# A fused Perceiver block: the scan stage's accumulation, gates and the next group's preparation moved to other rounds

## The reference

```
# 1 cross attention, 16 heads of 16, 256 keys of ctx per sequence, with a key mask, then x @ Wproj + bproj
# 2 Mamba block on the result
xn = layernorm(x);  xz = xn @ in_proj_w.T;  xi, z = xz[..., :512], xz[..., 512:]
xc = silu(causal depthwise conv of 4 taps(xi) + conv_b)
xp = xc @ x_proj_w.T                       # 1 dt column, 16 of B, 16 of C
delta = softplus(xp[..., :1] * dt_w + dt_b)
h_t = exp(delta_t * A) * h_{t-1} + delta_t * B_t * xc_t      # 512 channels x 16 states, 64 steps
y   = sum over states of h_t * C_t, + xc * D_skip
x   = x + (y * silu(z)) @ out_proj_w.T
# 3 feed-forward, 1024 inside, weights in {-1, 0, 1} times a scale, activations rounded to 8-bit steps per row
```

## Time and profile before

| | |
|---|---|
| Median of 3 runs | 426.24 us (425.74, 426.24 and 870.03) |
| Profiled execution | 425.23 us, of which the span of instructions is 423.4 us |
| Scan stage (first scan to last) | 191.7 to 371.4 us of the span |
| TensorE busy / ScalarE / VectorE / GpSimd | 364.6 / 276.4 / 350.2 / 280.5 us |
| Chain that ended last | PE 34%, DVE 28%, issue 15%, ACT 11%, POOL 10% |
| TensorE's granted clock, mean | 0.976 of full |

### The profile page before, as it was taken

The page is one execution under the profiler, slowest core; times in us unless marked ns, Lnnn a source line. Parts: engine busy times, 40 slices in busy tenths (PEclk is TensorE's granted clock), DMA queues, the critical chain, the costliest instruction groups (busy, mean ns, idle before and its releaser), DMA issues.

```text
span 423.4 us, 8649 instructions
## 1 busy us (share of the span) xinstructions
PE 364.6 (86%) x2868; PEld 246.3 (58%) x2868; DVE 350.2 (83%) x727; ACT 276.4 (65%) x592; POOL 280.5 (66%) x329
## 2 busy tenths in 40 slices
PE   3899999979998999887779889799889788789784
PEld 1556767666666764453446556464667566647443
DVE  1559889777898878859998999787899999988795
ACT  1267599659966982698765496838764665166564
POOL 0055566555748471449986779988799799986830
PEclk9999999999999999998998899989899999999989
DMA  6971011010100000049100000464000000000001
GB/s 200 395 303 52 2 50 52 2 50 2 52 2 0 3 2 0 2 115 267 21 2 0 2 2 28 133 151 116 0 2 2 0 2 0 2 0 2 12 26 63
DMA packets 22623, 22.41 MB, mean 53 GB/s; under 512 B 1042, under 2 KB 20242, under 8 KB 22068
## 3 DMA queue, kind: packets, MB, share of 16 engines
q1 hardware_dynamic: 22020, 21.39, 16.3%
q10 hardware_dynamic: 560, 0.48, 0.3%
HBM read 20.75 MB, written 1.12 MB: 52 GB/s over the span
## 4 chain that ended last, share of the span: by engine, by line
PE 34%; DVE 28%; issue 15%; ACT 11%; POOL 10%; DMA 1%; DVEq 1%; POOLq 0%; PEldq 0%; ACTq 0%
DVE both L1570 12%; PE ps L531 7%; POOL both L1865 6%; PE ps L745 4%; PE ps L500 3%; PE ps L735 3%; PE ps L483 3%; DVE xc L1536 2%; DVE both L1402 2%; PE ps L518 2%; PE ps L561 2%; ACT both L1000 2%; PE ps L548 2%; PE ps L704 2%; ACT both L1146 1%
## 5 line engine op out<-in xcount | busy, mean ns | idle before, releaser
L1865 POOL TENSOR_TENSOR both<-both 128x1024 f32<-128x1024 f32 x64 | 149.8, 2362 | 18.6 <-PE ps L745 12.5
L1570 DVE TENSOR_TENSOR_SCAN both<-both,ps 128x1024 f32<-128x1024 f32 x64 | 143.0, 2272 | 5.7 <-PE ps L735 5.7
L1811 POOL TENSOR_SCALAR both<-both,rden 128x256 f32<-128x256 f32 x128 | 61.7, 497 | 62.7 <-DVE rden L1409 62.6
L1160 ACT ACTIVATE both<-delta,a_neg 128x504 f32<-128x504 f32 x120 | 74.7, 704 | 10.9 <-DVE both L1570 10.9
L745 PE MATMUL ps<-con,both 128*128 128x128 f32 x512 | 74.5, 289 | 2.0 <-POOL both L1865 1.9
L1000 ACT ACTIVATE both<-both,negmax 128x256 f32<-128x256 f32 x128 | 63.3, 498 | 17.4 <-DVE negmax L1402 17.4
L745 PEld LDWEIGHTS ps<-con,both 128*128 128x128 f32 x512 | 58.1, 146 | 24.0 <-issue 19.2
L735 PE MATMUL ps<-both 32*128 32x256 f32 x512 | 47.2, 439 | 16.1 <-DVE both L1570 14.1
L1402 DVE CUSTOM_DVE_ANT_0 both<-ps,both 128x256 f32<-128x256 f32 x128 | 46.9, 418 | 6.7 <-PE ps L483 5.5
L735 PEld LDWEIGHTS ps<-both 32*128 32x128 f32 x512 | 20.6, 187 | 34.3 <-DVE both L1570 24.3
L531 PE MATMUL ps<-both 128*128 128x512 f32 x64 | 33.5, 648 | 8.0 <-DMA both<-in_ctx_t 6.6
(11 more groups left out here) (145 smaller groups left out, 603.4 us busy)
## 6 DMA issues: line engine op xcount, KB each, us to landing
both<-bounce SPq DMA_DIRECT2D x16, 512.0 KB, 5.5
both<-in_ctx_t SPq DMA_DIRECT2D x8, 512.0 KB, 3.4
both<-in_wg SPq DMA_DIRECT2D x1, 1024.0 KB, 8.5
both<-in_wu SPq DMA_DIRECT2D x1, 1024.0 KB, 10.9
both<-in_wd SPq DMA_DIRECT2D x1, 1024.0 KB, 12.9
win_sb<-in_win SPq DMA_DIRECT2D x1, 1024.0 KB, 14.8
resid<-in_x SPq DMA_DIRECT2D x1, 896.0 KB, 6.4
both<-in_wkv SPq DMA_DIRECT2D x1, 512.0 KB, 4.2
```

What stands on the lines that cost most here:

```text
L1160: act.activation(da[sl % 2].rearrange("p (a s n t) -> p a s n t", a=GT, n=HN, s=2)[:, :, :, n, 1:L], delta[:, idx % RING_D].rearrange("p ( ...
L1570: dve.tensor_tensor_scan(h_sb[:, hu % RING_H], da[e.slot % 2][:, e.tt * HU:(e.tt + 1) * HU], bank(inflow_bank(hu), 2), 0.0, ALU.mult, ALU. ...
L1811: pool.tensor_scalar(s, s, rden[:, u, q:q + 1], 1.0, ALU.mult, ALU.mult).then_inc(normed, 1)
L1865: pool.tensor_tensor(g_sb[:, hu % RING_G].rearrange("p (n s t) -> p s n t", n=HN, s=2), h_sb[:, hu % RING_H].rearrange("p (s n t) -> p s n ...
```

## The change

`LAG_ACC` goes from 5 to 4, and with it each accumulate stands one half earlier. In round k TensorE now has accumulate(2k - 4), in halves around phase 1 of the inflow, and accumulate(2k - 3) at the very end of the round, behind the projection; in a round with k % 4 == 1 (`block_ends`) the latter comes ahead of the projection. In a next_block round nothing stands between the two phases; `seed` and the whole accumulate(2k - 4) follow them. The gate goes behind scan 8i + 10 (hu % 8 == 2), where it was behind 8i + 11. VectorE's `u_of(3)` goes from behind scan 12 to behind scan 0, `convolve(1, 2)` and `(1, 3)` from behind 13 and 17 to 11 and 13, `copy_b` from 24 to 22, `u_of(4)` and `u_of(5)` from 26 and 34 to 28 and 35. TensorE's and ScalarE's work for group 1 moves with them. No computation is added or removed.

```diff
--- before.py
+++ after.py
@@ -57,7 +57,7 @@
 RING_H, RING_G, RING_X, RING_D = 4, 4, 6, 5
 INFLOW_BANKS = (2, 6, 0)
 Y_BANK, SPARE_BANK = 5, 4
-LAG_ACC = 5
+LAG_ACC = 4
 NT_ACT = 3
 
 
@@ -837,19 +837,23 @@
             project(t7)
             turn_u(0, 6, (z_sb, 1))
             for k in range(NB):
+                next_block, block_ends = k > 2 and k % 4 == 2, k % 4 == 1
                 inflow(k, 0)
                 if k == 1:
                     pe.wait_ge(z_late, count(1))
                     seed(0, (0, 1))
                 elif k == 2:
                     seed(0, (2, 3))
-                elif k > 2:
+                elif k > 2 and not next_block:
                     accumulate(2 * k - LAG_ACC, range(0, HN // 2))
                 inflow(k, 1)
-                next_block = k > 2 and k % 4 == 2
-                if k > 2:
+                if next_block:
+                    seed(k // 4, range(GT))
+                if next_block or k == 2:
+                    accumulate(2 * k - LAG_ACC)
+                elif k > 2:
                     accumulate(2 * k - LAG_ACC, range(HN // 2, HN))
-                if k >= 2 and not next_block:
+                if k > 2 and block_ends:
                     accumulate(2 * k - LAG_ACC + 1)
                 if k == 0:
                     turn_u(1, 1, (masked, NT * 16))
@@ -864,26 +868,26 @@
                     turn_u(2, SPARE_BANK, (conv_step, convolved(1, 0)))
                 if k == 4:
                     in_proj(1, 1, SPARE_BANK, (ut_act, 1))
+                if k == 5:
+                    in_proj(1, 2, SPARE_BANK, (conv_step, convolved(1, 1)))
                 if k == 6:
-                    in_proj(1, 2, SPARE_BANK, (conv_step, convolved(1, 1)))
+                    in_proj(1, 3, SPARE_BANK, (conv_step, convolved(1, 2)))
                 if k == 7:
-                    turn_u(3, SPARE_BANK, (conv_step, convolved(1, 2)))
-                if k == 8:
-                    in_proj(1, 3, SPARE_BANK, (ut_act, 2))
-                if k in (10, 11):
-                    x_proj(1, 2 * (k - 10), SPARE_BANK, (conv_step, convolved(1, 3)))
-                    x_proj(1, 2 * (k - 10) + 1, SPARE_BANK, (conv_step, convolved(1, 3)))
+                    turn_u(3, SPARE_BANK, (conv_step, convolved(1, 3)))
+                if k in (8, 9):
+                    x_proj(1, 2 * (k - 8), SPARE_BANK, (ut_act, 2))
+                    x_proj(1, 2 * (k - 8) + 1, SPARE_BANK, (ut_act, 2))
+                if k == 11:
+                    turn_b(1, SPARE_BANK, (bsb_ready, 2))
                 if k == 12:
-                    turn_b(1, SPARE_BANK, (bsb_ready, 2))
+                    in_proj(1, 4, SPARE_BANK, (bt_sb, 2))
                 if k == 13:
-                    in_proj(1, 4, SPARE_BANK, (bt_sb, 2))
+                    in_proj(1, 5, SPARE_BANK, (z_sb, NC))
                 if k == 14:
-                    turn_u(4, SPARE_BANK, (z_sb, NC))
+                    turn_u(4, SPARE_BANK, (z_sb, NC + 1))
                 if k == 15:
-                    in_proj(1, 5, SPARE_BANK, (ut_act, 3))
+                    in_proj(1, 6, SPARE_BANK, (ut_act, 3))
                 if k == 16:
-                    in_proj(1, 6, SPARE_BANK, (z_sb, NC + 1))
-                if k == 17:
                     in_proj(1, 7, SPARE_BANK, (z_sb, NC + 2))
                 if k == 18:
                     turn_u(5, SPARE_BANK, (z_sb, 2 * NC - 1))
@@ -913,10 +917,8 @@
                     turn_input(0, SPARE_BANK)
                 if k == 31:
                     turn_input(1, SPARE_BANK)
-                if next_block:
-                    seed(k // 4, range(GT))
+                if k >= 2 and not block_ends:
                     accumulate(2 * k - LAG_ACC + 1)
-            accumulate(NHU - 5)
             accumulate(NHU - 4)
             gates(0)
             up(0)
@@ -1224,29 +1226,30 @@
             silu_gates(0, slice(2, GT))
             tap_first(1)
             slot(3)
+            tap_first(2)
             half_slot(4, 0)
-            tap_first(2)
+            tap_first(3)
             half_slot(4, 1)
             copy_ut(3, SPARE_BANK)
-            half_slot(5, 0)
-            tap_first(3)
-            half_slot(5, 1)
             for c in range(NC):
                 silu_xc(1, c)
+            slot(5)
+            copy_pr(1, SPARE_BANK)
             slot(6)
-            copy_pr(1, SPARE_BANK)
-            slot(7)
             softplus(1, range(NC), dtb[:], (dt_loaded, 16))
+            half_slot(7, 0)
             copy_gates(1, 0, SPARE_BANK)
-            stage_xc(4, (z_sb, NC + 1 - 1))
+            half_slot(7, 1)
+            copy_gates(1, 1, SPARE_BANK)
+            stage_xc(4, (z_sb, NC + 2 - 1))
             half_slot(8, 0)
             copy_ut(4, SPARE_BANK)
             half_slot(8, 1)
-            copy_gates(1, 1, SPARE_BANK)
             copy_gates(1, 2, SPARE_BANK)
-            slot(9)
+            half_slot(9, 0)
             copy_gates(1, 3, SPARE_BANK)
             stage_xc(5, (z_sb, 2 * NC - 1))
+            half_slot(9, 1)
             silu_gates(1)
             copy_ut(5, SPARE_BANK)
             slot(10)
@@ -1709,15 +1712,14 @@
                 scan(hu)
                 if hu == 0:
                     copy_late_gate()
-                if hu == 12:
                     u_of(3)
-                if hu in (5, 9, 13, 17):
-                    convolve(1, (5, 9, 13, 17).index(hu))
-                if hu in (26, 34, 41, 49):
-                    u_of(NC + (26, 34, 41, 49).index(hu))
-                if hu % (NH * GT) == 3 and hu > NH * GT:
+                if hu % (NH * GT) == 2 and hu > NH * GT:
                     gate(hu // (NH * GT) - 1)
-                if hu == 24:
+                if hu in (5, 9, 11, 13):
+                    convolve(1, (5, 9, 11, 13).index(hu))
+                if hu in (28, 35, 41, 49):
+                    u_of(NC + (28, 35, 41, 49).index(hu))
+                if hu == 22:
                     copy_b(1, SPARE_BANK)
                 if hu == 47:
                     add_scan(0, 0)
```

## The result

The changed kernel took 414.97 us, the median of 4 runs (414.41 to 417.95). The kernel before took 428.85 us beside it (425.74 to 870.03). The ratio is 0.9738, 95% interval [0.9701, 0.9774]: faster. It leaves out the single execution of 870.03 us, which lies far from all others; what lifts the median above the 426.24 us shown earlier is the fourth execution, of 431.46 us. The profiled execution took 414.41 us, its span 412.6 us, against 425.23 and 423.4.

The account below looks back on a forecast made before the run. The hand-written order was taken as the bound, VectorE's waits ahead of the first statistics as the gain: 16.0 - 5.6 - 0.6 = 9.8, less 0.9 for the clock, 8.9 off 425.23, plus 0.7 to the median: 417.0 us, range 412.5 to 424.

Parts of the forecast that it names:

- The waits removed: On VectorE, gate waits (2.3 us), first tap (0.8), u_of(4) (3.13) and u_of(5) (2.56) go; ceiling of gain 16.0 us.
- The waits put in: Ahead of VectorE's scans: waits of 5.0 us left, 5.6 with 0.1 for each of six.
- The walk: Rounds from scan 4 on, timed with measured start-to-start times; sum 16.0 - 5.6 - 0.6 = 9.8 us gained.
- Scan 4: Early scan stage: scan 4 keeps its place at 201.8; u_of(3) fills the 0.60 us ahead, leaving 0.2.
- TensorE's clock: Rounds 6, 7 and 14: new idle times may bring 1.2 GHz stretches, 0 to 4 us; 0.9 taken off.
- What a halved stretch costs: Behind idle times of rounds 6, 7 and 14: 1.0 to 1.5 us, of which round 14's would count whole.
- The end follows the first statistics: From 87.4 us ahead of the end: the end moves as much as the statistics while GpSimd waits for them.
- VectorE beside GpSimd: u_of(3) beside GpSimd's spread of B: between 0 and 0.6 us lost, 0 taken; by the skill's exclusion up to 0.6.
- More than counted: Rival, chance 0.13: projections hide behind convolutions and gates, round 14 is covered; 3 of 5.6 us vanish: 413.5.
- Half of it comes back: Rival, chance 0.30: TensorE's waits in rounds 6, 7, 14 and a later GpSimd hold up phase 1; 5 us less, 421.5.
- the wall: Rival, chance 0.06: GpSimd's weighs rather than VectorE set the end; time stays near 425.5.
- the clock rival: Rival, chance 0.05: in rounds 5 to 19, halved projection rounds take 10 us against 4.4; three eat the gain, two more give 434.

Follow-up runs that it names:

- Experiment 4: The changed kernel with u_of(4) behind scan 27 instead of 28, nothing else: 413.17 us, ratio 0.9705.
- experiment 10: The changed kernel with u_of(4) behind scan 27, offset_input(0) and (1) behind weigh 50 and 52, and L1653's scaling on ScalarE: 410.78 us, ratio 0.9654.
- experiment 8: The changed kernel with offset_input(0) and (1) behind weigh 50 and 52 and L1653's 2-element scaling on ScalarE instead of VectorE: 411.49 us, ratio 0.9644.
- experiment 1: The kernel before with only the new order (lag 4, gate, seed); group 1's preparation left where it was: 422.67 us, ratio 0.9898.
- experiment 3: The kernel of experiment 1 plus two filler matmuls, read by nothing, ahead of phase 0 in rounds 6 and 10: 421.15 us, ratio 0.9876.
- experiment 5: The changed kernel plus an unread 1.2 us VectorE reduction behind scan 49, ahead of the first statistics: 415.76 us, ratio 0.9755.
- experiment 6: The changed kernel plus an unread 1.2 us VectorE reduction behind scan 57, after the first statistics: 416.36 us, ratio 0.9768.
- experiment 7: The changed kernel with GpSimd's offset_input(0) and (1) behind weigh 50 and 52 instead of 48 and 50: 414.42 us, ratio 0.9713.
- experiment 9: The changed kernel with L1653's three 2-element scalings on ScalarE and nothing else: 416.3 us, ratio 0.9748.
- experiment 2: The kernel before with only group 1's preparation moved; lag 5, gate behind scan 8i + 11 and seed position kept: 421.62 us, ratio 0.9892.

## Why the prediction was right, step by step

417.0 us was forecast, within 412.5 to 424.0; 414.97 came. The mechanism was right and the sum before its corrections nearly exact; one correction charged 0.9 us for something that did not come, and one step was right only for the size of gain in question.

- **The waits removed.** Gates, the first tap, u_of(4) and u_of(5): all as told. u_of(4) was due at 268.3 and ran at 268.27 without a wait, its xc staged at 264.94. dt was asked for at 248.99 and softplus began at 253.73:

```profile
253.73 2.93 ACT L1138 ACTIVATE delta<-dtb,vec 128x512 f32<-128x512 f32 x4
264.94 0.60 ACT L1178 ACTIVATE ps<-xc 128x512 f32<-128x512 f32 x1
```

- **The waits put in.** Forecast 0.6, 0.5, 1.4, 0.7, 0.7 and 0.9 at scans 18, 26, 30, 32, 34 and 46; measured 0.59, 0.46, 1.39, 0.59, 0.59 and 0.95. (The terms printed for round 22, the last of them, add up to 6.0 and not 5.9.) Scan 30's is released as the walk said: TensorE idles for u_of(4), and turn and accumulate stand ahead of inflow. Experiment 4 takes it away and gets 1.3 us.

```profile
269.08 0.63 PE L692 MATMUL ps<-con,u_sb 128*128 128x128 f32 x4 [1.45 <-DVE u_sb L1594]
269.54 1.04 PE L745 MATMUL ps<-con,both 128*128 128x128 f32 x8
270.51 0.71 PE L735 MATMUL ps<-both 32*128 32x256 f32 x8
```

- **The walk.** Scan 34 was put at 282.7 and began at 282.63, scan 50 at 322.5 and began at 322.24; GpSimd's wait for statistics was to end at 326.1 and ended at 325.84. The sum of 9.8 us became 10.11.
- **Scan 4.** The walk left it at 201.8, and it began at 201.85, but for another reason. The stage began 1.4 us sooner (scan 0 at 190.28, before at 191.72), and scan 4 waited 1.45 us under a halved clock (0.50 at 198 to 199), behind four matmuls of in_proj that took 3.78 us. The early start and the wait cancel out: here the forecast was right by luck. Of the seven profiled executions of experiments 4 to 10, which share this part, six have no wait at scan 4, and experiment 8's has 1.51 us, again with a long stretch at the halved clock.
- **TensorE's clock, the step that failed.** I took 0.9 us off the gain for new stretches at the halved clock. There were none behind scan 4. TensorE did stop in rounds 6, 7 and 14, as counted (1.46, 1.22 and 1.45 us), and what came behind ran at full speed: the accumulate of round 14 took 1.04 us. Old stretches went: added up over stretches of one microsecond (186 to 376), the granted clock stood at the 1.2 GHz level for some 17 us before and some 7 after, and TensorE's 364.6 us busy became 357.3. The kernel before had five such stretches: one ahead of scan 4, which is the one left, two behind the stops of 2.05 us for a gate, and two behind stops of 2.43 and 1.54 us for a scan (222 to 227, 236 to 240). That they went needed no term of its own, since what they cost was in the waits that the walk took out (the two of 1.26 us, and probably part of gate(0)'s 1.33, where most other gates waited 0.45). So the correction should have been nothing.
- **What a halved stretch costs** was undersized as well: I put 1.0 to 1.5 us, and the one of experiment 1 (244 to 250, longer than that of 274 to 278 behind gate(2)) cost 2.93 at scan 22, as experiment 3 shows. The Trainium skill (TensorE: Matmul & The Clock Gate, "Part 1: The HAM clock gate") has the slow clock as what the engine falls to when it is not kept busy; experiments 1 and 3 agree, with 2.43 us of idle ahead of the halving, and 0.71 us and no halving when filler stood in it. The length of the last stop alone does not decide: 2.44 us in round 6 of experiment 1 and 2.03 us in the kernel before (ahead of 247.18) were followed by full speed, 1.54 us there (ahead of 235.07) by the halved clock.
- **The end follows the first statistics.** It did, to 0.02 us at the last weigh, and experiment 5 confirms it for a delay. But it holds only while GpSimd waits, as the prediction said, and VectorE's own list behind the statistics is as late as GpSimd's, as it did not say: experiments 6, 7 and 9. The tail gave 0.65 us more, with a granted clock of 0.99 in it against 0.96. That goes with the execution and not, as far as the runs show, with the change: from gate(7) to the end the changed kernel took 44.67 us and experiments 1, 2, 4 and 7 took 44.66 to 44.72, while the kernel before and experiments 3, 5 and 6 took 45.26 to 45.37, and of these nine just the last four have a stretch at the 1.2 GHz level 25 to 28 us behind gate(7). (Experiments 8 and 10 took 45.00 and 44.96, experiment 9 46.85.)
- **VectorE beside GpSimd.** u_of(3) cost VectorE nothing (0.68 us, the next scan directly behind it). GpSimd paid: one spread took 1064 ns, where the longest of the 16 took 661 in the kernel before and 667 in experiment 1, which leaves u_of(3) behind scan 12. So the exclusion that the prediction quotes shows here, at GpSimd's expense; the 0.45 us did not reach the end, since GpSimd waited 1.85 us for a scan soon after, at 210.76 (duration ns min/median/max, starts us):

```profile
L1855 POOL TENSOR_TENSOR both<-con,bt x16: 604/613/1064, 183.7 to 279.4; 128x256 f32<-128x256 f32 x16
```

The place where the two engines exclude each other is L1653 (the earlier trace rows before): 1.61, 0.21 and 0.83 us in the changed kernel, twice ending with a weigh. The 0.21 us fell into GpSimd's L1902, which did not hold them up (second fence below).

```profile
335.98 1.61 DVE L1653 TENSOR_SCALAR f_s<-wmean,f_s 128x2 f32<-128x2 f32 x1
...
342.57 0.21 DVE L1653 TENSOR_SCALAR f_s<-wmean,f_s 128x2 f32<-128x2 f32 x1
...
361.31 0.83 DVE L1653 TENSOR_SCALAR f_s<-wmean,f_s 128x2 f32<-128x2 f32 x1
```

```profile
342.32 1.07 POOL L1902 TENSOR_SCALAR dtb<-xnt 128x256 bf16<-128x256 f32 x1
```

- **From execution to median.** I added 0.7; 0.56 was measured. So 425.23 - 10.11 - 0.65 + 0.56 = 415.0: the 2.0 us between forecast and time are the 0.9 of the clock, 0.65 of the tail, 0.3 of the walk and 0.15 here.
- **The rivals.** "More than counted" named a gain near 413.5 by hidden projections; they were not hidden (0.59 each), so that mechanism is out although the time lies between it and the forecast. "Half of it comes back" did not happen to the change: ahead of the statistics no half accumulate waited for a weigh, and no stretch was halved behind scan 4. It is the halves of the change in experiments 1 and 2 that lost to halved stretches. GpSimd was not the wall, and with experiment 10 it is: from 240 to the last weigh it waits 0.4 us there. The price of the clock rival does not add up: at its 5.6 us a round, five rounds cost 28 us and not the 17 that lead to 434.

## What to carry to other kernels

In a pipeline written in order, walk the steps engine by engine with measured start-to-start times: it gave six waits to 0.11 us each, and missed the seventh, at scan 4, by 1.25 us. Price a stop of TensorE not by its length but by what stands behind it at half the clock, look in the trace whether the clock fell there at all, and look whether a move closes old stops before charging it for new ones. Where two engines arrive together at the same point, a gain on one is worth little until the other is relieved as well (0.75 and 0.03 us alone, 3.68 together).

## What the runs showed of the hardware

- Two useless matmuls in one round made the wait at scan 22 2.93 us shorter, because TensorE kept 2.4 GHz (experiment 3). Idle times of 2.43 and 3.65 us stood ahead of halved stretches; of 1.45 us (turn_u(4) in the changed kernel), 2.03 us (kernel before) and 2.44 us (experiment 1, round 6) they were followed by full-speed matmuls. So the same length of stop can go either way.
- A `tensor_scalar` on VectorE over 128x2 float32 values took 0.21 us beside GpSimd's L1902 and 0.83, 1.61, 2.01 and 2.40 us beside GpSimd's multiplications, each time ending within 0.1 us of the end of one. The Trainium skill (SBUF — State Buffer, "Who interferes with whom") says that a `tensor_scalar` can enter a mode in which it and GpSimd's instruction exclude each other as a whole; the 2.40 us agree with it, the 0.21 us inside the 1.07 us of L1902 do not (how exact GpSimd's recorded times are is not known). The scans and the products with one input in PSUM kept their 2.2 and 1.2 us beside the same multiplications.
- A `tensor_tensor` on VectorE with both inputs in SBUF, u_of(3), kept its 0.68 us, and the GpSimd instruction beside it took 1.06 us instead of 0.61.
